# A graph network on one core: new order of the steps in the two attention passes

## What is computed

```python
def gat_conv(x, src, dst, W, a_src, a_dst, b):
    h = (x @ W).reshape(N, HEADS, HEAD_DIM)
    alpha_s = jnp.einsum('nhc,hc->nh', h, a_src)
    alpha_d = jnp.einsum('nhc,hc->nh', h, a_dst)
    e = alpha_s[src] + alpha_d[dst]
    e = jnp.where(e > 0, e, NEG_SLOPE * e)
    m = jax.ops.segment_max(e, dst, num_segments=N)
    ex = jnp.exp(e - m[dst])
    denom = jax.ops.segment_sum(ex, dst, num_segments=N)
    alpha = ex / (denom[dst] + 1e-16)
    msg = h[src] * alpha[:, :, None]
    out = jax.ops.segment_sum(msg, dst, num_segments=N)
    return out.reshape(N, HEADS * HEAD_DIM) + b
```

## Time and profile before

| | us |
|---|---|
| median of 3 runs | 8629.59 (8629.22 to 8640.47) |
| the profiled execution | 8623.56, of which the profile's span is 8621.7 |
| pass 1, first difference to the last line of the pass | about 5946 to 7211 of the span |
| pass 2, the same | about 7377 to 8586 of the span |
| busy over the span | PE 6160.1, DVE 5075.3, POOL 4101.0, ACT 2537.0 |

### The profile page before, as it was taken

The page is one execution under the profiler, slowest core; times in us unless marked ns, Lnnn a source line. Parts: engine busy times, 40 slices in busy tenths (PEclk is TensorE's granted clock), DMA queues, the critical chain, the costliest instruction groups (busy, mean ns, idle before and its releaser), DMA issues. The chain is left out here.

```text
span 8621.7 us, 114948 instructions
## 1 busy us (share of the span) xinstructions
PE 6160.1 (71%) x25212; PEld 4605.7 (53%) x25213; DVE 5075.3 (59%) x9533; ACT 2537.0 (29%) x5700; POOL 4101.0 (48%) x4374
## 2 busy tenths in 40 slices
PE   3877778765366666699999999955666665577775
PEld 1446666654144444366666666633555553455554
DVE  4248888873433332266666666665666666566666
ACT  0135555542200000233333333333333332233332
POOL 0036666640077775043444444414666661666663
PEclk9988878878577787699999999976777777677777
DMA  3257777771033333143443443423444441544443
GB/s 117 112 182 230 234 234 234 232 208 37 18 105 105 105 105 80 45 125 111 119 120 113 119 120 111 120 55 117 127 135 134 125 133 45 150 137 139 138 139 94
DMA packets 440460, 1100.92 MB, mean 128 GB/s; under 512 B 102512, under 2 KB 177365, under 8 KB 439479
## 3 DMA queue, kind: packets, MB, share of 16 engines
q0 software_dynamic: 249344, 763.23, 31.6%
q1 hardware_dynamic: 190636, 333.56, 11.7%
HBM read 1014.51 MB, written 81.94 MB: 127 GB/s over the span
## 5 line engine op out<-in xcount | busy, mean ns | idle before, releaser
L765 POOL DMA_INDIRECT st_rows<-g_table,st_stage_idx x1632 | 1561.5, 957 | 861.4 <-issue 459.1
L2429 PE MATMUL st_psM<-st_msg,st_hot 128*128 128x273 f32 x3264 | 962.4, 456 | 265.3 <-DVE st_msg L2276 265.3
L859 POOL DMA_INDIRECT st_rows<-kv_table,st_stage_idx x832 | 846.7, 1018 | 482.1 <-issue 233.5
L705 POOL DMA_INDIRECT st_rows<-p_table,st_stage_idx x816 | 841.8, 1032 | 302.9 <-issue 220.3
L2429 PEld LDWEIGHTS st_psM<-st_msg,st_hot 128*128 128x128 f32 x3264 | 714.4, 224 | 469.2 <-issue 161.9
L765 POOL DMA_INDIRECT st_rows<-h_table,st_stage_idx x816 | 775.9, 951 | 244.4 <-issue 236.3
L1555 DVE TENSOR_TENSOR st_pre<-st_psP,st_rows 128x512 f32<-128x512 f32 x816 | 524.0, 683 | 536.5 <-PE st_psP L1646 393.4
L1652 PE MATMUL st_psC<-st_w,st_rT 128*128 128x256 f32 x3264 | 815.0, 393 | 0.0
L1652 PEld LDWEIGHTS st_psC<-st_w,st_rT 128*128 128x128 f32 x3264 | 587.5, 190 | 373.8 <-ACT st_rT L1613 212.3
L1462 PE MATMUL st_psM<-st_rows,st_hot 128*128 128x256 f32 x1632 | 500.1, 475 | 385.1 <-DMA st_rows<-h_table,st_stage_idx 188.3
L1608 ACT ACTIVATE st_gate<-st_pre 128x256 f32<-128x256 f32 x816 | 340.4, 417 | 1288.0 <-DVE st_pre L1555 1287.8
(11 more groups left out here) (399 smaller groups left out, 11737.0 us busy)
## 6 DMA issues: line engine op xcount, KB each, us to landing
st_dst_row<-in_dst_row SPq DMA_DIRECT2D x310, 512.0 KB, 5.6
kv_table<-st_rows_out SPq DMA_DIRECT2D x25, 1560.0 KB, 5.6
st_ea<-in_ea SPq DMA_DIRECT2D x103, 256.0 KB, 3.8
st_rows<-g_table,st_stage_idx POOLq DMA_INDIRECT x1632
st_pens<-pen_table SPq DMA_DIRECT2D x208, 72.0 KB
st_rows<-kv_table,st_stage_idx POOLq DMA_INDIRECT x832, 5.0
st_rows<-h_table,st_stage_idx POOLq DMA_INDIRECT x816
st_rows<-p_table,st_stage_idx POOLq DMA_INDIRECT x816, 3.7
```

The source lines that it names most:

```text
L705: pool.indirect_dma_start(out=rows[:, u * SLOTS + j, :], out_offset=None, in_=table, in_offset=bass.IndirectOffsetOnAxis(ap=stage_idx[:, u ...
L765: pool.indirect_dma_start(out=rows[:, slot, j, :], out_offset=None, in_=table, in_offset=bass.IndirectOffsetOnAxis(ap=stage_idx[:, g, u * ...
L859: pool.indirect_dma_start(out=rows[:, slot, j, :], out_offset=None, in_=kv_table, in_offset=bass.IndirectOffsetOnAxis(ap=stage_idx[:, g, u ...
L2429: last = nc.tensor.matmul(out[:, 0:MSG_W], onehots[:, j, :], msg[:, n, j, :], start=(j == 0), stop=(j == SLOTS - 1))
```

## The change

It does these things, all of them in `gat_pass`:

- DVE's `group` is cut in two halves. The first does `messages` 0 and 1, combine 0, then `edge_scores` of the next group, then `messages` 2. The second does combine 1, `segment_maxima`, combine 2 and then the difference of the next group (`differences`). `edge_scores` stood between `messages` 0 and 1 before, combine 1 behind `segment_maxima`, and the difference at the head of the group.
- `diff` has two buffers, and ACT makes the weights of the next group at its own group's end, behind the factors of combine 2 and ahead of the extras' one-hot rows. ACT's third `hotrow` moves behind the factors of combine 1.
- PE's `turn_scores` moves behind scatter 1.
- `work_of` is cut into `blocks_of` (two numbers) and `extras_of` (the other two, loaded only where there is an extra). DVE loads the blocks of a group's three supertiles at once, between `messages` 0 and 1.
- A matrix product with two columns of zeros ends each `expand` and alone raises `expanded`; DVE needs no number of extras to wait for any more.
- The row of column numbers that `one_hot` compares with is read from SBUF (`iota_row`) and not from a copy in PSUM (`columns`).

```diff
+    def extras_of(eng, row):
+
+        _, values = nc.values_load_multi_w_load_instructions(
+            work[0:1, ds(row, 1), 0:2].squeeze(1), engines=[eng.engine], min_val=-1, max_val=NS * NB,
+            skip_runtime_bounds_check_because=BOUNDED)
+        return at_least_zero(eng, values, NS * NB)
+
+    def blocks_of(eng, row, count=1):
+
+        _, values = nc.values_load_multi_w_load_instructions(
+            work[0:1, ds(row, count), 2:4], engines=[eng.engine], min_val=0, max_val=NS * NB,
+            skip_runtime_bounds_check_because=BOUNDED)
+        return [(values[2 * n], values[2 * n + 1]) for n in range(count)]
+
...
-                    def group(i, g, ahead):
+                    def differences(i, g):
                         q = 2 * i + g
+                        dve.wait_ge(S["back_ps"], START + q + 1)
+                        hold(dve, held)
+                        v.tensor_tensor(diff[:, g, :, :, :], et[:, :, :, :], group_view(psW), ALU.subtract).then_inc(S["diffed"], 1)
+
+                    def first_half(i, g, ahead):
                         s = 6 * i + U * g
                         link.turn()
-                        dve.wait_ge(S["back_ps"], START + q + 1)
-                        v.tensor_tensor(diff[:, :, :, :], et[:, :, :, :], group_view(psW), ALU.subtract).then_inc(S["diffed"], 1)
                         messages(i, g, 0)
+                        blocks = blocks_of(dve, s + 1, U)
+                        messages(i, g, 1)
+                        combine(s, g % 2, s + U, 0, blocks[0])
                         if ahead:
-                            dve.wait_ge(S["diffed"], START + q + 1)
+                            dve.wait_ge(S["diffed"], START + 2 * i + g + 1)
                             edge_scores(i + g, 1 - g)
-                        messages(i, g, 1)
-                        combine(s, g % 2, s + U, 0)
                         messages(i, g, 2)
+                        return blocks
+
+                    def second_half(i, g, ahead, blocks):
+                        s = 6 * i + U * g
+                        combine(s + 1, (g + 1) % 2, s + U + 1, 1, blocks[1])
                         if ahead:
                             segment_maxima(i + g, 1 - g)
-                        combine(s + 1, (g + 1) % 2, s + U + 1, 1)
-                        combine(s + 2, g % 2, s + U + 2, 2)
+                        combine(s + 2, g % 2, s + U + 2, 2, blocks[2])
+                        if ahead:
+                            differences(i + g, 1 - g)
...
+                    def weights(i, g):
+                        act.wait_ge(S["diffed"], START + 2 * i + g + 1)
+                        hold(act, held)
+                        nc.scalar.activation(group_view(psU), diff[:, g, :, :, :], ACT.Exp).then_inc(S["weights"], 1)
+
+                    def group(i, g, ahead, last=False):
                         q = 2 * i + g
                         s = 6 * i + U * g
-                        act.wait_ge(S["diffed"], START + q + 1)
-                        nc.scalar.activation(group_view(psU), diff[:, :, :, :], ACT.Exp).then_inc(S["weights"], 1)
                         message_columns(i, g, 0)
                         message_columns(i, g, 1)
                         make_factors(s)
...
                         message_columns(i, g, 2)
                         if ahead:
                             make_hotrow(q + 2, 1)
+                        make_factors(s + 1)
+                        if ahead:
                             make_hotrow(q + 2, 2)
-                        make_factors(s + 1)
                         make_factors(s + 2)
+                        if not last:
+                            weights(i + g, 1 - g)
                         if ahead:
                             make_extra_hotrows(q + 2)
...
-                        bring(hotrow[:, u, :, :], block_number(b0), u == 0).then_inc(S["expanded"], 1)
+                        bring(hotrow[:, u, :, :], block_number(b0), u == 0)
                         with pe.If(more):
+                            x0, x1 = extras_of(pe, s + 1)
                             with pe.Fori(x0, x1) as x:
                                 pe.wait_ge(S["x_hotrow"], START + x + 1)
                                 bring(xhotrow, block_number(b0 + 1 + x - x0), False).then_inc(S["x_expanded"], 1)
+                        at = u * 2 * H3
+                        nc.tensor.matmul(psE[:, at:at + 2], hotrow[:, u, 0, :], zeros[:, :], start=False, stop=True,
+                                         skip_group_check=True).then_inc(S["expanded"], 1)
...
                         scatter_extra(s, g % 2)
+                        scatter(s + 1, 1, (g + 1) % 2)
                         if next_scores:
                             turn_scores(q + 1)
-                        scatter(s + 1, 1, (g + 1) % 2)
```

More of the change, by code:

```diff
@@ L2141, in gat_pass @@
             psZ = st.ps("psZ", [P, 512])
-            columns = psU[:, 512 - P:512]
             lanes = psX[0:LANES, :]
@@ L2212, in make_hot @@
                     def make_hot(s, u):
-                        one_hot(hot[:, u, :, :], dst_of(s), columns).then_inc(S["onehot"], 1)
+                        one_hot(hot[:, u, :, :], dst_of(s)).then_inc(S["onehot"], 1)
                     def raise_max(sums, b, count):
@@ L2229, in add_scaled, with combine, take_extra @@
                         v.tensor_tensor(at, at, part[:, :].rearrange("p (h c) -> p h c", h=H3), ALU.add).then_inc(count, 1)
-                    def combine(s, n, ahead, ahead_u):
-                        x0, x1, b0, more = work_of(dve, s + 1)
+                    def combine(s, n, ahead, ahead_u, block):
+                        b0, more = block
                         def next_block():
                             link(v.tensor_scalar(rel[:, :], rel[:, :], -float(P), None, ALU.add))
-                            one_hot(xhot[:, :, :], rel[:, :], columns).then_inc(S["x_onehot"], 1)
-                        def take_extra(x):
+                            one_hot(xhot[:, :, :], rel[:, :]).then_inc(S["x_onehot"], 1)
+                        def take_extra(x, x0):
                             b = block_number(b0 + 1 + x - x0)
@@ L2315, in _ @@
                     segment_maxima(0, 0)
+                    differences(0, 0)
                     with dve.Fori(0, TURNS - 1) as i:
                         for g in range(2):
-                            group(i, g, True)
-                    group(TURNS - 1, 0, True)
-                    group(TURNS - 1, 1, False)
+                            blocks = first_half(i, g, True)
+                            second_half(i, g, True, blocks)
+                    blocks = first_half(TURNS - 1, 0, True)
+                    second_half(TURNS - 1, 0, True, blocks)
+                    blocks = first_half(TURNS - 1, 1, False)
+                    second_half(TURNS - 1, 1, False, blocks)
                 @block.scalar
@@ L2398, in _ @@
                         make_extra_hotrows(q)
+                    weights(0, 0)
                     with act.Fori(0, TURNS - 1) as i:
@@ L2402, in _ @@
                     for g in range(2):
-                        group(TURNS - 1, g, False)
+                        group(TURNS - 1, g, False, g == 1)
                 @block.tensor
```

31 lines of the change are left out of this document (17 added, 14 removed).

## The result

The changed kernel takes 8683.49 us (median of 4 runs, 8682.67 to 8690.24), the kernel before beside it 8629.4: a ratio of 1.0063, interval 1.0045 to 1.008. The profiled execution took 8690.24, 67 us more than the 8623.56 of before. Foretold was 8572, with a range from 8490 to 8650: the sign was wrong, and the time lies outside the range.

What follows compares the result with a forecast made beforehand. No engine is full; VectorE's waits in a chain that changes engines bound it. Pass 2 -18, pass 1 -33, starts and tails -11, SBUF one-hots and second loads +5: -57, 8567 profiled, median 6 above: 8572 us, range 8490 to 8650.

Steps and rivals of the forecast that it cites:

- The start of scatter 0: TensorE's first scatter, timed from the scan's end: 10.0 us with an extra prepared, about 6.6 without.
- the third kind of group: Groups with an extra in combine 2 and another prepared: 40.6 us foretold, 37.6 before.
- The extras' rows: ACT's one-hot rows for a prepared extra: start 5.5 us behind the scan's end, against 6.85 before.
- the first kind of group: Groups with an extra prepared and an extra in combine 1: 37.4 us foretold, 27.8 before.
- rival 3: No net gain: extras' rows start at 6.85 us, not 5.5; 1.35 us in 44 groups, 8631; 0.18 shared with rival 2.
- An extra in combine 2: VectorE's one-hot 1.5 us, wait for its scatter 3.1, the rest 2.66: 7.4 in all, difference at 10.2.
- the fourth group: Group with a jump back, an extra prepared and one in combine 0: 11.3 + 6.1 + 13.9 + 3.75 = 35.1 us, 40.5 before.
- TensorE's expand: With no extra prepared, PE expands without waiting and is free at about 6.6 us; VectorE goes on at 12.7.
- The part behind scatter 0: VectorE's combine 0, scores, messages 2, combine 1, scans: 13.9 us with gaps, 9.8 before; 4.1 us of work moved there.
- rival 4: Slower: ACT's factors of combine 1 come late behind two hotrows; 8717 at 3.5 us late; chance 0.14.
- Rival 2: VectorE's jump back changes price with the loop's place: 8518 (0.22, shared) or 8631 (0.18, shared with rival 3).
- One-hot from SBUF: VectorE's one_hot reading SBUF: between -0.02 and +0.02 us for 250 of them, at most 5 us.

Runs made afterwards that it cites:

- e7: The changed kernel with the extras' one-hot rows ahead of combine 2's factors on ScalarE: 8619.62 us, 0.9991 of before.
- e5: The changed kernel with the extras' one-hot rows ahead of combine 2's factors, and TensorE's expand of two supertiles earlier: 8585.37 us, 0.9951 of before.
- e17: The kernel before with only the early difference (two buffers) and weights ahead of the extras' rows: 10138.78 us on a slower chip, 0.9923 of before.
- e9: e5 with the semaphore for the next dst_row transfers raised later, behind message_columns 1 of the next group: 8529.83 us, 0.9887 of before.
- e6: The kernel before with the extras' one-hot rows ahead of combine 2's factors on ScalarE: 8579.93 us, 0.9943 of before.
- e10: e9 with the loops of VectorE, ScalarE and TensorE turned, so jumps back lie near the wait for scatter 0: 8372.08 us, 0.9709 of before.

## Why the prediction was wrong, point by point

- **The start of scatter 0: the step that failed.** The forecast lets it start at 10.0 us with an extra prepared, at 20.3 in the third kind of group, and without an extra prepared at 6.6, or at 8.6 behind pass 2's jump. It started at 11.4, at 22.6, and at 8.1 to 8.3, or 9.4 to 10.1: some 65 us in all, and so the wait's end came no sooner, or too little, to pay for the 4.1 us moved. The next four points are its parts. e7 and e5 show that rows and expand are what holds scatter 0.
- **The extras' rows.** "Those rows start at ... 5.5", with "an estimate between 0 and 0.6" for one more register load. In the first kind of group it is 6.6 to 6.9. The loads of three supertiles, and a second one for the extra, stand between weights and rows where nothing hides them: 3.25 us, 1.43 more than with single loads (e17). This is rival 3, given a part of 0.18 and priced at 1.35 us in 44 groups, 8631. By its cause it happened in the first kind of group, and its price leaves 52 us of the measured time open.
- **An extra in combine 2.** The forecast prices it at 7.4 us; it cost 9.0 in the mean of 16 groups, 25 us in all. The wait for its scatter was taken at 3.1 us from one row of before and is 4.3 in the mean, since the scatter takes longer and starts later. The 0.32 us that the forecast takes off ahead of the difference also came back (0.35). Besides, its own terms give 10.2 + 0.35 + 2.3 = 12.85 for the next rows, not 12.6, and the 11.3 of the fourth group is worked out nowhere.
- **TensorE's expand.** "PE is free at about 6.6" was 8.0 to 8.3: it starts 2.3 to 2.8 us behind the scan and takes 1.93 a supertile.
- **ScalarE's own jump back** (2.86 us above, 3.47 in another turn) was in no term; scatter 0 waits 0.6 to 1.5 us for it in pass 2's turns without an extra prepared.
- **The part behind scatter 0.** 4.1 us moved was right, but 13.9 is 14.3 to 14.6, with 0.2 us gaps ahead of the scores, the one-hot and the scans, and groups with an extra in it are 0.3 to 2.1 us above their sum: 43 us in 64 groups, more than any one of the parts above.
- **What was right.** The waits for weights (13.6 us over both passes), rows and scores; the jump's 3 us in pass 2; combine 1's factors, which came in time (rival 4 didn't happen). In pass 1 most jumps were 5.3 to 6.5 us and not 7.8, 20 to 30 us better than foretold; that was luck, and without it the miss would have been larger.
- **Rival 2.** The jump's price changes, but by what the DMA queues carry at that moment (e7, e9), not by the loop's place alone. The Trainium skill's page "Runtime: NRT & Kernel Launch", section "Instruction fetch mechanics", has a taken branch wait for a fetch when its target lies outside the two blocks held; the traces agree, with instruction packets in every such idle time, and with a second one in pass 1.
- **One-hot from SBUF.** VectorE's cost was zero as foretold. That it would make another engine slower was not thought of: 49 ns on 1632 gathers, 80 us of GpSimd's time, off the path here. The Trainium skill's page "GPSIMD Engine Reference", section "1. Specifications", says that GpSimd contends with VectorE instructions that have two SBUF inputs. The one-hot is one of these now, and was none with a row in PSUM; the traces agree.

## What to carry to other kernels

Before work is moved behind the wait that ends last, ask whether what ends this wait comes sooner by at least as much; here it came no sooner in the groups of the first kind (17.9 us against 18.0), for 4.1 us moved. A wait copied from one row of before is a price at that row's clock and that row's neighbours: the extra's scatter took 6.5 us in the mean and not 5.75. Work that depends on nothing new (one-hot rows, expands) belongs ahead of the steps that everything waits for, and a loop's jump back into a stretch where its engine waits anyway. A transfer that is let go earlier can lie ahead of an instruction fetch: look at what a moved semaphore sets off.

## What the chip showed

- A jump back of VectorE cost 2.9 to 3.9 us in pass 2, 4.3 to 7.9 with three transfers of dst_row sent up to 4 us ahead of it (e5, e6, e7), and 5 to 12 in the loop of pass 1, where a second packet of instructions comes late.
- A gather on GpSimd that meets a one-hot with two SBUF inputs can take twice its time. In e10 the 390 gathers that overlap one take 1187 ns in the mean and the others 950; in the kernel before, with the row in PSUM, 947 and 960. From e10:

```profile
8141.32 0.94 POOL L779 DMA_INDIRECT st_rows<-g_table,st_stage_idx  x1 [0.30 <-issue]
8142.42 1.21 DVE L763 TENSOR_TENSOR st_hot<-dst_rel,iota_row 128x1024 f32<-128x1024 f32 x1
8142.56 1.89 POOL L779 DMA_INDIRECT st_rows<-g_table,st_stage_idx  x1 [0.30 <-issue]
```

- The same program, the kernel before, took 8626 us on some chips and 10220 to 10406 on others, at a mean granted clock of 0.81 to 0.82 and 0.76 to 0.77. An order that gained 2.9% on the one kind gained less than half of that, 1.0 to 1.2% (with the row in PSUM), on the other.
